# Turning the queries of each pair's second chunk with VectorE's 32x32 blocks and transfers through memory

## What is computed

```python
x_norm = layernorm(layernorm(x)) * ln_g + ln_b
q, k, v = split(x_norm @ W_qkv)
gate = sigmoid(layernorm(x) @ W_gate); gate = gate / (mean(gate) + EPS)
q = relu(q * gate) ** 2 + EPS          # 16 heads of 32 columns
k = relu(k * gate) ** 2 + EPS
for t in range(2048):                   # per batch and head
    kv = kv + outer(k[t], v[t]); ks = ks + k[t]
    o[t] = (q[t] @ kv) / (q[t] . ks + EPS)
x = x + o @ W_proj
x = x + gelu(layernorm(x) @ U1 @ V1 + b1) @ U2 @ V2 + b2
```

## Time and profile before

| | before |
|---|---|
| median of three runs | 1697.15 us (1697.0 to 1698.67) |
| the profiled execution | 1697.67 us |
| its span in the trace | 1695.9 us |
| PE busy | 1665.1 us, 98% |
| DVE busy | 1400.3 us, 83% |
| ACT busy | 630.5 us, 37% |
| POOL busy | 900.2 us, 53% |
| clock granted to PE, mean | 0.996 |

### The profile page before, as it was taken

One profiled execution on the slowest core, in us unless ns is written; L12 is line 12 of the kernel. 1 busy time (PEld: TensorE's weight loads), 2 busy tenths in 40 slices (PEclk: granted clock), 3 DMA queues, 4 the chain that ended last, 5 costly groups with the idle time before them and its releaser, 6 DMA issues.

```text
span 1695.9 us, 39553 instructions
## 1 busy us (share of the span) xinstructions
PE 1665.1 (98%) x16221; PEld 1401.9 (83%) x16221; DVE 1400.3 (83%) x2223; ACT 630.5 (37%) x1178; POOL 900.2 (53%) x1026
## 2 busy tenths in 40 slices
PE   6899999999999999999999999999999999999998
PEld 4688888888888888888888888888888888888876
DVE  6888888888888888888888888888888888888875
ACT  4233333333333333433433333333333333333332
POOL 3355555555555555555555555555555555555540
PEclk9999999999999999999999999999999999999999
DMA  8323323333322333342333233343223323322210
GB/s 231 88 58 70 59 75 46 72 75 57 72 72 45 74 70 60 73 71 47 74 72 59 73 62 56 74 69 61 74 49 69 75 57 70 74 45 73 58 45 26
DMA packets 206324, 115.67 MB, mean 68 GB/s; under 512 B 151144, under 2 KB 161792, under 8 KB 206144
## 3 DMA queue, kind: packets, MB, share of 16 engines
q1 hardware_dynamic: 205280, 111.57, 31.4%
q10 hardware_dynamic: 864, 1.57, 0.5%
HBM read 79.38 MB, written 33.72 MB: 67 GB/s over the span
## 4 chain that ended last, share of the span: by engine, by line
PE 93%; DVE 3%; DMA 1%; issue 1%; SPq 1%; ACT 0%; POOL 0%; DVEq 0%; POOLq 0%
PE ps_a L849 11%; PE ps_a L850 10%; PE ps_a L851 10%; PE scores L849 8%; PE scores L851 8%; PE scores L850 8%; PE ps_h L849 4%; PE ps_h L850 4%; PE ps_h L851 4%; PE scores L980 4%; PE scores L1008 4%; PE ps_q L849 3%; PE ps_q L850 3%; PE ps_q L851 3%; PE scores L856 3%; PE ps_a L1026 2%
## 5 line engine op out<-in xcount | busy, mean ns | idle before, releaser
L447 POOL TENSOR_TENSOR h_lo<-h_full,h_hi 128x512 fp32r<-128x512 f32 x244 | 336.4, 1389 | 220.4 <-DVE h_hi L665 219.0
L849 PE MATMUL ps_a<-wx_hi,zt_hi 128*128 128x512 f32 x768 | 315.7, 411 | 6.3 <-DVE key_sums L787 4.2
L850 PE MATMUL ps_a<-wx_lo,zt_hi 128*128 128x512 f32 x768 | 305.1, 397 | 0.0
L851 PE MATMUL ps_a<-wx_hi,zt_lo 128*128 128x512 f32 x768 | 305.0, 397 | 0.0
L530 ACT ACTIVATE h_full<-ps_h,cols 128x256 f32<-128x256 f32 x512 | 204.5, 476 | 144.1 <-PE ps_h L851 137.6
L849 PEld LDWEIGHTS ps_a<-wx_hi,zt_hi 128*128 128x128 f32 x768 | 145.3, 189 | 43.2 <-DVE zt_lo L620 7.1
L665 DVE CAST h_hi<-h_full 128x512 fp32r<-128x512 f32 x256 | 163.3, 648 | 17.8 <-ACT h_full L530 13.7
L851 PEld LDWEIGHTS ps_a<-wx_hi,zt_lo 128*128 128x128 f32 x768 | 145.1, 189 | 35.6
L850 PEld LDWEIGHTS ps_a<-wx_lo,zt_hi 128*128 128x128 f32 x768 | 145.3, 189 | 28.7 <-issue 0.5
L541 ACT ACTIVATE query_t<-scores 128x512 f32<-128x512 f32 x64 | 38.3, 599 | 345.9 <-PE scores L856 345.9
L467 POOL TENSOR_TENSOR key_lo<-keys,key_hi 128x512 fp32r<-128x512 f32 x64 | 86.9, 1358 | 121.1 <-ACT key_hi L561 121.1
(11 more groups left out here) (156 smaller groups left out, 4230.7 us busy)
## 6 DMA issues: line engine op xcount, KB each, us to landing
xs<-L_attn_x SPq DMA_DIRECT2D x64, 256.0 KB, 4.1
key_blocks<-zs SPq DMA_DIRECT2D x64, 256.0 KB, 2.0
key_t<-key_blocks SPq DMA_DIRECT2D x256, 64.0 KB
out<-x1s SPq DMA_DIRECT2D x64, 256.0 KB, 2.1
xt<-x_turned SPq DMA_DIRECT2D x63, 256.0 KB, 4.2
key_sums<-carry_rows SPq DMA_DIRECT2D x60, 256.0 KB, 3.7
rows<-turned_rows SPq DMA_DIRECT2D x63, 64.0 KB, 4.5
x1s<-L_attn_W_gate SPq DMA_DIRECT2D x4, 256.0 KB, 4.2
```

Of the source, the lines that this page charges most:

```text
L447: E.tensor_tensor(h_lo[:, i % SLOTS, :], h_full[:, i % SLOTS, :], h_hi[:, i % SLOTS, :].bitcast(F32), ALU.subtract).then_inc(s["h_lo_ready ...
L849: E.matmul(ps, wh, mh, start=start and i == 0, stop=False)
L850: E.matmul(ps, wh, ml, start=False, stop=False)
L851: mm = E.matmul(ps, wl, mh, start=False, stop=stop and i == last)
```

## The change

For second chunks only (`half` 1), TensorE's four query transposes and ScalarE's copy to `query_t` are gone. Instead VectorE transposes the divided queries by blocks of 32x32 into `probs[:, 1, :]`, right behind count 6 of `den_steps` and ahead of the residual sum. SP, behind `carry_rows`, waits for that (`qry_ready`), writes the 256 KB to a new tensor in memory (`query_blocks`), waits until they have landed (`qry_out`), and issues four transfers of 64 KB, in pieces of 128 bytes, that fill `query_t`. TensorE's scores of such a chunk wait for these four (`query_t_in`) in place of `query_t_ready`. First chunks keep their way; their semaphore counts now go by pairs (`c.pair()`).

```diff
--- before.py
+++ after.py
@@ -58,6 +58,10 @@
         self.first = m is not None and m < BATCHES
         self.row = (p + off // 4) * P
 
+    def pair(self, per=1):
+
+        return per * ((4 * self.p + self.off) // 2 + 1)
+
     def done(self, per=1, i=1):
 
         return self.p * (4 * per) + (per * self.off + i)
@@ -106,7 +110,7 @@
 
 
...
@@ -205,7 +209,7 @@
...
-            sums_done den_steps blocks_ready blocks_out tq_done query_t_ready
+            sums_done den_steps qry_ready qry_out blocks_ready blocks_out tq_done query_t_ready
...
@@ -213,6 +217,7 @@
         s = {n: sem(n) for n in names}
         x_in = [sem(f"x_in{i}") for i in range(4)]
         xt_in = [sem(f"xt_in{i}") for i in range(4)]
+        query_t_in = [sem(f"query_t_in{j}") for j in range(HPG)]
         key_t_in = [sem(f"key_t_in{j}") for j in range(HPG)]
         rows_out = [sem(f"rows_out{i}") for i in range(4)]
         rows_in = [sem(f"rows_in{i}") for i in range(4)]
@@ -365,6 +370,17 @@
                     sp.wait_ge(s["den_steps"], c.done(6, 2))
                     sp.dma_start(carry_dram[c.slot:c.slot + 1, :], key_sums[P - 1:P, :])\
                         .then_inc(carry_out[c.slot], 16)
+                if c.exists and c.half:
+
+                    sp.wait_ge(s["qry_ready"], c.pair())
+                    for j in range(HPG):
+                        wait(sp, query_t_in[j], c.pair(16) - 16)
+                    sp.dma_start(qry_dram, probs[:, 1, :]).then_inc(s["qry_out"], 16)
+                    sp.wait_ge(s["qry_out"], c.pair(16))
+                    for j in range(HPG):
+                        sp.dma_start(query_t[j * HEAD:(j + 1) * HEAD, :, :].rearrange("d f (a t) -> d f a t", t=HEAD),
+                                     qry_dram.rearrange("(a d) (f j t) -> j d f a t", d=HEAD, f=KT, t=HEAD)[j])\
+                            .then_inc(query_t_in[j], 16)
                 after = Chunk(p, b + 1)
                 if after.exists and not after.first:
 
@@ -536,8 +552,8 @@
                 n, c, d = Chunk(p, b), Chunk(p, b - 1), Chunk(p, b - 2)
                 ffn = Group(p, (b - 3) // 2) if b % 2 else Group(p, (b - 4) // 2)
                 pairs = range(4) if b % 2 else range(4, 8)
-                if c.exists:
-                    act.wait_ge(s["tq_done"], c.done())
+                if c.exists and c.half == 0:
+                    act.wait_ge(s["tq_done"], c.pair())
                     E.activation(query_t[:, :, :].rearrange(flat), ps_t[:, :], ACT.Copy)\
                         .then_inc(s["query_t_ready"], 1)
                 if n.exists:
@@ -716,10 +732,12 @@
                             E.tensor_tensor(x1s[:, r.slot, :], ps[:, :], x1s[:, r.slot, :], ALU.add)\
                                 .then_inc(s["result_ready"], 1)
                 if n.exists:
-                    if c.exists:
-                        dve.wait_ge(s["tq_done"], c.done())
+                    if not c.exists:
+                        add_rows(1)
+                    elif c.half:
+                        dve.wait_ge(s["qry_ready"], c.pair())
                     else:
-                        add_rows(1)
+                        dve.wait_ge(s["tq_done"], c.pair())
                     squared_relu(n, s["query_done"], s["query_steps"], ps_a, QUERY, queries[:, :])
                 if b % 2 and ffn.exists:
                     dve.wait_ge(s["pt_hi_ready"], ffn.done())
@@ -805,6 +823,10 @@
                     E.scalar_tensor_tensor(out=by_head, in0=by_head, scalar=EPS,
                                            in1=den[:, 2, :].unsqueeze(2).broadcast_to([P, NH, HEAD]),
                                            op0=ALU.add, op1=ALU.mult).then_inc(den_steps, 1)
+                    if n.half:
+
+                        dve.wait_ge(den_steps, n.done(6, 6))
+                        E.transpose(probs[:, 1, :], queries[:, :]).then_inc(s["qry_ready"], 1)
                 if c.exists:
 
                     dve.wait_ge(s["y_done"], c.done())
@@ -934,8 +956,8 @@
                 if d.exists:
                     pe.wait_ge(s["z1_ready"], d.done())
 
-                    if c.exists:
-                        pe.wait_ge(s["query_t_ready"], c.done())
+                    if c.exists and c.half == 0:
+                        pe.wait_ge(s["query_t_ready"], c.pair())
                     else:
                         pe.wait_ge(s["probs_ready"], d.done())
                     transpose4(zs, s["tx_done"])
@@ -969,7 +991,11 @@
                         pe.wait_ge(s["x1_steps"], d.done(3, 1))
                     for j in range(HPG):
                         pe.wait_ge(key_t_in[j], c.done(16, 16))
-                    pe.wait_ge(s["query_t_ready"], c.done())
+                    if c.half:
+                        for j in range(HPG):
+                            pe.wait_ge(query_t_in[j], c.pair(16))
+                    else:
+                        pe.wait_ge(s["query_t_ready"], c.pair())
                     if d.exists:
                         pe.wait_ge(s["x1t_ready"], d.done())
                     if result is not None and result.exists:
@@ -1067,8 +1093,9 @@
...
+    qry_dram = nc.dram_tensor("query_blocks", (P, DM), _mybir.dt.float32, kind="Internal").ap()
-    block_kernel(nc, *args, out, carry_dram, rows_dram, blocks_dram)
+    block_kernel(nc, *args, out, carry_dram, rows_dram, blocks_dram, qry_dram)
```

More of the change, by code:

```diff
@@ L108, in block_kernel @@
 def block_kernel(nc, x, ln_g, ln_b, w_qkv, b_qkv, w_gate, b_gate, w_proj, b_proj,
-                 u1, v1, b1, u2, v2, b2, x_turned, out, carry_dram, rows_dram, blocks_dram):
+                 u1, v1, b1, u2, v2, b2, x_turned, out, carry_dram, rows_dram, blocks_dram, qry_dram):
     ctx = ExitStack()
```

## The result

The changed kernel takes **1709.03 us** (median of 4 runs, 1703.63 to 1711.74), the kernel before, on the same chip, 1697.08 us (4 runs, 1694.59 to 1698.67). The ratio is 1.0068, with a 95% interval of 1.004 to 1.0096: slower by 0.7%, where the forecast was 0.2% faster. The profiled execution took 1703.63 us, the shortest of the four, with a span of 1701.9 us and a mean granted clock of 0.996, as before.

A forecast was written before the change was run, and what follows sets the result against it. TensorE, busy for 98% of the span, was taken as the bound; -12.9 + 2.5 + 5 + 1.5 = -3.9 us against 1697.15 gave 1693.2 us (chance 0.33), range 1686.5 to 1714.

The forecast's parts named there:

- What it adds on VectorE: Behind the divided queries, VectorE gets 0.73 us more per second chunk; KEY's cover and VectorE's idle 1.69 us absorb it.
- What it removes: Between GATE and KEY, TensorE loses four transposes: 0.43 us a pair, 12.9 us over 30 pairs.
- fifth rival: VectorE becomes the bound as its 0.73 us aren't absorbed: at most 9 us lost; within the no-change case, chance 0.24.
- On the way of the queries: Through memory to the scores, queries land 0.88 us early in the pair read; 2.5 us of waiting over 30 pairs.
- first rival: The four query reads take 8.2 us, 2.1 us late in each pair: +62, 1759 us; chance 0.13.
- First pair: At the first second-chunk scores, queries come 5.2 us late behind carry_rows; taken as 5 us, from 3 to 7.
- Last pair: At the last pair's scores, with nothing queued, queries come 1.5 us late, from 0.5 to 4.
- The rules of the Trainium skill: For the query transfers, they say the turn should stay with TensorE and the transfers would not hide, as in the first rival.
- second one: Rival: the queue is held up 1 us longer than carry_rows shows, 18 us of waits: +12, 1709 us; chance 0.20.

The follow-up runs named there:

- bare: The changed kernel without VectorE's query transpose, the write, the four reads and the wait for them; 1686.09 us, ratio 0.9937.
- pool_late: The changed kernel with GpSimd's add of the projection's bias to xs moved behind the centring of xt in even steps; 1691.74 us, ratio 0.997.
- turn_no_transfer: The changed kernel without the write, the four reads and TensorE's wait for them, VectorE's transpose kept; 1706.06 us, ratio 1.0061.
- gap: The changed kernel with VectorE's transpose moved behind the statistics' aggregation (line 844), into its wait for GpSimd's statistics; 1698.39 us, ratio 1.0005.
- ends_pool: pool_late with the queries of chunks 1 and 63 turned by TensorE again; 1689.97 us, ratio 0.9952.
- ends_old: The changed kernel with the queries of chunks 1 and 63 turned by TensorE again, nothing else; 1703.29 us, ratio 1.0042.
- turn_added: The kernel before with VectorE's transpose of the divided queries added, its result unused, TensorE's transposes kept; 1707.07 us, ratio 1.0057.
- first_swap: pool_late with SP's write of the means' 4-byte pieces moved behind the reads of key_t in the second step alone; 1695.38 us, ratio 0.9991.

## Why the prediction was wrong

**The step that failed** stands in "What it adds on VectorE": "So the delay ends there, and VectorE's idle 1.69 us ahead of line 696 takes it up." Of VectorE's own row that is right. Line 712 starts on the gate's scale 5.20 us behind the queries, sooner than before (5.37), and the idle time ahead of it fell to 0.79. What I didn't follow is the other engine that hangs on the delayed residual sum: GpSimd's statistics and adds move by 0.73 us, no idle time on that side takes it up, and VectorE's instruction on the keys is held until the end of the add. So the shift reaches the probabilities whole (0.75 us, 13.92 to 14.67). There the slack was 0.44 us, and the change itself had taken 0.43 of it by making TensorE faster; I had looked at what TensorE needs in the scores' step only. Price: a pair of 51.60 instead of 50.86 us, 0.74 x 29 = 21 us at the most, against the 12.9 that TensorE gave.

Point by point:
- *What it removes*, 0.43 us a pair: right. bare has pairs of 50.88 us against 51.32, and is 11 us faster by the medians.
- *On VectorE*: the transpose took 0.71 us; KEY didn't wait for it. The rest as above. My fifth rival, VectorE's 0.73 us not absorbed, was the right place with a wrong bound and a wrong reason: "at most 9 us of the 12.9 lost". The bound held TensorE's wait per pair at 0.3 us and left out that a gain of TensorE makes the same wait longer.
- *On the way of the queries*: right, and it had most of my attention. Write issued 0.03 us behind the transpose; landed 3.1 us after that, 2.7 predicted; scores never waiting in the middle. The reads landed 4.3 to 5.3 us after the first issue, 4.4 in the median, where 5.2 was taken and 8.2 was the first rival's. SP's waits over the run:

```profile
SPq L389 <- DMA carry_rows<-key_sums: 97.3, 30, 4.3
SPq L381 <- DMA query_blocks<-probs: 84.6, 32, 3.6
```

  The 84.6 us over 32 are 2.6 a pair, within the 2 to 3.5 predicted. The 2.5 us of TensorE's waits that I had counted in the middle didn't come.
- *First pair*: 5 predicted, 5.7 measured, and pool_late shows that the transfers alone would give it. But half the story was missing, since the lock and the late write give nearly as much without them: turn_no_transfer is 4.7 us above the kernel before there, and TensorE waited for the transfers for 1.1 us only. That the number came out is in good part luck.
- *Last pair*: 1.5 predicted, 0.89 measured (7.41 us from the queries to the scores against 6.52 in the earlier trace rows). The reads took 4.4 us and not 5.2. TensorE stood idle for just 0.11 us there, as `zs` was late by VectorE's transpose too and its own work ended at nearly the same time.
- *The rules of the Trainium skill against transfers in small pieces* (DMA: Bandwidth & Descriptors, section Specifications) *and against a plain transfer that does the transposing* (VectorE: DVE Perf Modes, section The three transpose paths): in the middle of this kernel they cost nothing where they start right behind VectorE's transpose; in gap, 1.4 us later, they cost 4.8 us of waits. With transfers and without VectorE's turn the kernel is at 1689.1 us, without both at 1686.1, and the 60 steps in the middle take 1522.0 and 1522.8 us; the difference lies outside them.
- *The rivals*: the time fell on the second one's 1709, by another mechanism, and within the range, which reached to 1714. That is luck: the rival and the upper end of the range stood on waits for late queries in the middle pairs, and none came.

The sum with the measured terms: -12.9 + 21 (less 0.64 for each short pair) + 5.7 + 0.9 = +15 with no short pair and +10 with eight; the medians say +12. The trace with its eight short pairs is only 6 us longer than the one before, mostly because the stretches ahead of the first scores and behind the last were 1.6 and 1.4 us shorter in it.

**What beats both kernels** is ends_pool: VectorE and memory turn the queries in the middle, TensorE at both ends, and GpSimd's add comes later. 1689.97 us, 0.48% below the kernel before, some 4 us above bare. Its six runs lie at 1686.0 to 1687.9 and at 1692.1 to 1693.0; the two lengths of the first pair (20.6 and 26.3 us) would explain that, but only one profile of it exists, so this is not shown. Nor is it settled why ends_old's median fell by 5.7 us when its trace gives only 0.8 at the first pair and 1.1 at the last. That trace is of an execution of 1708.75 us, 5.5 above its kernel's median, so it doesn't speak for the others; how often each kernel has which first pair stays open.

## What to carry to other kernels

An instruction put into one engine's queue delays everyone who hangs on what stands behind it: follow each of them to its end, not just the engine's own next idle time. Where two engines can lock each other out, ask of a shift which instructions it brings together, and price the end of the other's instruction rather than the length of one's own. And a saving on the bounding engine uses up the slack of all who deliver to it; list these slacks (here 0.44 us) before counting the saving.

## What the runs showed of the hardware

- A 128x512 instruction of VectorE with both inputs in SBUF and one of GpSimd shut each other out: 0.75 becomes 1.90 us, or 1.30 becomes 1.85. The blocked time is counted as busy, not as a wait. With VectorE's start 0.05 to 0.07 us ahead, and GpSimd's previous add still running, GpSimd won 21 times in 29; with the add 0.04 to 0.14 us ahead, in all 29 (turn_added).
- 128 pieces of 4 bytes in SP's queue hold up a 256 KB write issued just ahead of them. In the first pair the write lands after 8.6 to 11.8 us in the eleven traces in which the pieces are issued 1.4 to 3.1 us behind it, and after 3.2 to 4.6 us in the three in which they come 3.5 us behind it or later (before, turn_added, first_swap).
- The granted clock falls to 0.50 (1.2 GHz) in the first pair of bare, where TensorE had just stood idle for 1.99 us. The trace is of bare's slowest execution, 1691.73 us. Windows with the engines' busy us, PEclk, DMA share and GB/s:

```profile
52.00:54.00 2.00, 0.24 (x8) 0.27 (x12) 1.93 (x4) 0.63 (x1) 1.09 (x2) 1.00 0.50 84
...
56.00:58.00 2.00, 2.00 (x6) 1.54 (x6) 1.28 (x1) 0.00 (x0) 1.21 (x1) 0.50 1.03 332
```

  Products follow each other after 0.43 us there instead of 0.23, until the clock is back at 1.00 (2.4 GHz) in the window from 60.
